# Two graph layers on one core: counts stored tile by tile, weights and count slabs on each other's queues, count ranges in pairs of chunks

## What is computed

```
edge_index = jnp.stack([src, dst])
x = _layernorm(x + graph_attention(x, W_fc, attn_l, attn_r, W_res, src, dst))
x = _layernorm(x + three_relational_layers(x, node_type, edge_index, edge_type, ...))

# attention, 12 heads of 64:   e = leaky_relu(a1[src] + a2[dst]); alpha = softmax of e over the edges of dst
#                              relu(x @ W_res + segment_sum(alpha * ft[src], dst))
# relational layer (3 times):  xw = h @ w_rel[r] for each relation r
#                              msg = xw[edge_type, src] / count[dst, edge_type]
#                              h = relu(segment_sum(msg, dst) + h @ w_root + bias)
```

## Time and profile before

| | |
|---|---|
| three runs | 2420.83, 2431.07, 2428.05 us; median 2428.05 |
| the profiled execution | 2421.66 us, span 2419.8 us |
| PE busy | 2181.1 us (90%) |
| DVE, ACT, POOL busy | 1225.3, 784.7, 461.4 us |
| moved by DMA | 215.26 MB in 138214 packets |
| mean granted TensorE clock | 0.959 |

### The profile page before, as it was taken

The page is one execution under the profiler, slowest core; times in us unless marked ns, Lnnn a source line. Parts: engine busy times, 40 slices in busy tenths (PEclk is TensorE's granted clock), DMA queues, the critical chain, the costliest instruction groups (busy, mean ns, idle before and its releaser), DMA issues.

```text
span 2419.8 us, 29974 instructions
## 1 busy us (share of the span) xinstructions
PE 2181.1 (90%) x10968; PEld 1835.2 (76%) x10969; DVE 1225.3 (51%) x1875; ACT 784.7 (32%) x1071; POOL 461.4 (19%) x389
## 2 busy tenths in 40 slices
PE   6999853888887599999999999999999899999997
PEld 2555531333333499999999899999999899999997
DVE  7888767999976633322322432322322342343335
ACT  1133334888885321211211421211211321212212
POOL 0000003999998000000000000000000000000000
PEclk8999975999998699999999999999999999999998
DMA  1134423211110433333432423333333423345332
GB/s 50 45 87 105 105 61 94 76 33 33 33 35 16 137 105 103 111 108 92 115 98 86 120 63 104 111 101 91 116 91 92 131 66 116 105 114 140 99 98 76
DMA packets 138214, 215.26 MB, mean 89 GB/s; under 512 B 87760, under 2 KB 87998, under 8 KB 138073
## 3 DMA queue, kind: packets, MB, share of 16 engines
q1 hardware_dynamic: 97187, 141.08, 20.7%
q0 software_dynamic: 40144, 70.00, 10.1%
q10 hardware_dynamic: 767, 2.57, 0.3%
HBM read 182.51 MB, written 30.70 MB: 88 GB/s over the span
## 4 chain that ended last, share of the span: by engine, by line
PE 59%; DMA 4%; DVE 3%; ACT 1%; issue 0%; ACTq 0%; DVEq 0%
PE banks L1193 30%; PE banks L1165 28%; DMA w_raw<-in_L_gnn_w_root_dram 4%; DVE w_lo L1413 1%; ACT w_hi L1295 1%; PE banks L1217 1%; PE banks L1204 0%; DVE norm_stats L1385 0%; DVE res L1381 0%; PE banks L1235 0%; DVE h_lo L1444 0%; ACT accT L1324 0%; DVE tail_stats L1464 0%; DVE back L1462 0%; ACT accT L1286 0%
## 5 line engine op out<-in xcount | busy, mean ns | idle before, releaser
L1165 PE MATMUL banks<-ct_in,h_hi 125*128 125x416 f32 (+1 forms) x1710 | 603.7, 353 | 0.6 <-ACT accT L1286 0.6
L1165 PE MATMUL banks<-ct_in,h_lo 125*128 125x416 f32 (+1 forms) x1710 | 602.5, 352 | 0.0
L1193 PE MATMUL banks<-g_hi,w_hi 128*128 128x416 f32 (+1 forms) x1440 | 516.5, 359 | 22.5 <-DVE g_lo L1435 22.5
L1193 PE MATMUL banks<-g_hi,w_lo 128*128 128x416 f32 (+1 forms) x1440 | 513.8, 357 | 0.0
L1193 PE MATMUL banks<-g_lo,w_hi 128*128 128x416 f32 (+1 forms) x1440 | 511.2, 355 | 0.0
L1413 DVE TENSOR_TENSOR w_lo<-w_raw,w_hi 128x768 fp32r<-128x768 f32 (+1 forms) x228 | 227.9, 1000 | 474.7 <-ACT w_hi L1295 474.7
L1295 ACT CAST w_hi<-w_raw 128x768 fp32r<-128x768 f32 (+1 forms) x228 | 198.0, 868 | 466.0 <-PE banks L1193 353.7
L939 PE MATMUL head_sums<-pw,x 125*65 125x512 f32 x720 | 274.2, 532 | 59.9 <-POOL pw L723 44.1
L1165 PEld LDWEIGHTS banks<-ct_in,h_lo 125*128 125x128 f32 x1710 | 323.1, 189 | 4.1
L1165 PEld LDWEIGHTS banks<-ct_in,h_hi 125*128 125x128 f32 x1710 | 321.7, 188 | 4.3 <-ACT accT L1286 0.8
L1311 ACT CAST g_hi<-gs 128x416 fp32r<-128x416 f32 (+3 forms) x180 | 97.4, 541 | 700.1 <-DVE gs L1423 700.1
(11 more groups left out here) (198 smaller groups left out, 1565.6 us busy)
## 6 DMA issues: line engine op xcount, KB each, us to landing
w_raw<-in_L_gnn_w_rel_dram SPq DMA_DIRECT2D x117, 384.0 KB, 3.1
ct_in<-s_ct POOLq DMA_DIRECT2D x18, 2031.2 KB, 28.2
w_raw<-in_L_gnn_w_rel_dram SPq DMA_DIRECT2D x54, 448.0 KB, 4.5
ct_in<-s_ct POOLq DMA_DIRECT2D x9, 2041.0 KB, 28.7
s_ct<-ct_stage SPq DMA_DIRECT2D x30, 610.4 KB
w_raw<-in_L_gnn_w_root_dram SPq DMA_DIRECT2D x39, 384.0 KB, 3.1
w_raw<-in_L_gnn_w_root_dram SPq DMA_DIRECT2D x18, 448.0 KB, 5.3
low_spread<-s_low SPq DMA_DIRECT2D x11, 610.4 KB
```

The lines of the kernel that those rows point to most:

```text
L1165: ins = nc.tensor.matmul(pb[0:rows, PA, 0:s.w], a, b, start=j == 0, stop=j == len(pairs) - 1)
L1193: ins = nc.tensor.matmul(pb[:, m, 0:s.w], a, b, start=s.first and j == 0, stop=s.last and j == len(parts) - 1)
```

## The change

It has three parts, in one diff.

1. Ranges begin at pairs of chunks. NPAIR = 160 pairs take the place of NRUN = 80 runs in the table. A pass of the loop still takes four chunks, now pairs q and q + 1, and the loop steps by 2; `ranges` rounds the number of pairs up to an even one, at least 2, with seven more small instructions. `oh_rem` is built in the same 20 instructions, with 2 in place of 4 as its innermost size. `hit` now lies in `csf`.
2. Counts are kept tile by tile: `dram["ct"]` is (R, NT, T, NT, T), relation, tile of destinations, partition, source tile, destination. A store writes 5000 contiguous bytes for each partition. A load of a slab is cut into PIECES = 4 transfers, one for each tile of destinations that the group touches; each still has 125 partitions by ten pieces of up to 125 numbers (500 bytes). All stores but those of the last tile are now issued in the count stage itself.
3. In the relational layers the queues are exchanged. POOL issues the weights, SP the slabs. SP stores four tiles of x1, then issues slab 0, stores four more, waits, issues slab 1, stores the last two; later each slab at the first step of the slab before it, in one order with the late loads and stores of x1.

```
@@ -27,9 +27,9 @@
...
-REM_R = 4
+REM_R = 8
...
-NRUN = NCH // CG
+NPAIR = NCH // 2
...
@@ -81,16 +81,16 @@
...
-        hit = sb("hits", [NW, 3, NRUN], F32)
-        rng = sb("ranges", [NW, 4], F32)
+        hit = csf[0:NW].rearrange("w s d -> w (s d)")[:, 0:3 * NPAIR].rearrange("w (m i) -> w m i", m=3)
+        rng = sb("ranges", [NW, 6], F32)
...
-        oh_rem = sb("oh_rem", [CH, NRUN, LANES, CG], BF16)
+        oh_rem = sb("oh_rem", [CH, NPAIR, LANES, 2], BF16)
...
@@ -134,10 +134,10 @@
...
-            return (nc.s_assert_within(eng.snap(both >> 7), 0, NRUN - 1, skip_runtime_bounds_check_because=WITHIN),
-                    nc.s_assert_within(eng.snap(both & 127), 1, NRUN, skip_runtime_bounds_check_because=WITHIN))
+            return (nc.s_assert_within(eng.snap(both >> 8), 0, NPAIR - 2, skip_runtime_bounds_check_because=WITHIN),
+                    nc.s_assert_within(eng.snap(both & 255), 1, NPAIR - 1, skip_runtime_bounds_check_because=WITHIN))
...
@@ -161,25 +161,24 @@
             with nc.allow_non_contiguous_dma(reason="100 numbers"):
                 sp.dma_start(tabf[:], rng[:, 2:3]).then_inc(tab_in, 16)
 
-            def tile(tt, b, kept=0):
+            def tile(tt, b, last=False):
                 g = tt * 2 + b
                 sp.wait_ge(rows_split, g * 2 + 2)
                 for m in range(2):
                     sp.dma_start(a_rows[m * H:(m + 1) * H, bass.ds(g * T, T)], splitrow[:, m]).then_inc(rows_out, 16)
-                if kept < R:
-                    tile_staged(sp, tt, b)
-                for r in range(R - kept):
-                    sp.dma_start(dram["ct"][r].rearrange("(s p) (u c d) -> p s u c d", p=T, c=2, d=T)[:, :, bass.ds(tt, 1), b].rearrange(
-                        "p s u d -> p s (u d)"), stage[0:T, b, r]).then_inc(stored[b], 16)
-                if not kept:
-                    sp.dma_start(dram["deg"][bass.ds(g, 1), :],
-                                 stage[T:T + 1, b].rearrange("a r s d -> a (r s d)")).then_inc(stored[b], 16)
+                if last:
+                    return
+                tile_staged(sp, tt, b)
+                for r in range(R):
+                    sp.dma_start(dram["ct"][r, bass.ds(g, 1)].rearrange("a p s d -> (a p) s d"), stage[0:T, b, r]).then_inc(stored[b], 16)
+                sp.dma_start(dram["deg"][bass.ds(g, 1), :],
+                             stage[T:T + 1, b].rearrange("a r s d -> a (r s d)")).then_inc(stored[b], 16)
 
             with sp.Fori(0, NT // 2 - 1) as tt:
                 tile(tt, 0)
                 tile(tt, 1)
-            tile(NT // 2 - 1, 0, kept=2)
-            tile(NT // 2 - 1, 1, kept=3)
+            tile(NT // 2 - 1, 0)
+            tile(NT // 2 - 1, 1, last=True)
             sp.wait_ge(rows_out, 32 * NT)
 
         @block.gpsimd
@@ -273,23 +272,35 @@
...
+                lo, hi, n = (rng[:, j:j + 1] for j in (0, 1, 4))
+                nc.vector.tensor_scalar(hi, rng[:, 2:3], 1.0, None, ALU.max).then_inc(dv, 1)
+                nc.vector.tensor_scalar(lo, rng[:, 3:4], -1.0, float(NPAIR), ALU.mult, ALU.add).then_inc(dv, 1)
...
+                nc.vector.scalar_tensor_tensor(out=lo, in0=hi, scalar=-1.0, in1=lo, op0=ALU.add, op1=ALU.min).then_inc(dv, 1)
...
+                nc.vector.tensor_tensor(n, hi, lo, ALU.subtract).then_inc(dv, 1)
...
+                nc.vector.tensor_scalar(n, n, 0.5, 0.25, ALU.mult, ALU.add).then_inc(dv, 1)
...
+                nc.vector.tensor_scalar(n, n, MAGIC, None, ALU.add).then_inc(dv, 1)
...
+                nc.vector.tensor_scalar(n, n, -MAGIC, 2.0, ALU.add, ALU.mult).then_inc(dv, 1)
...
+                nc.vector.tensor_tensor(hi, hi, n, ALU.max).then_inc(dv, 1)
...
+                nc.vector.tensor_tensor(lo, hi, n, ALU.subtract).then_inc(dv, 1)
...
+                nc.vector.scalar_tensor_tensor(out=rng[:, 2:3], in0=lo, scalar=256.0, in1=hi,
...
-                                        rem16[:, i * CG:(i + REM_R) * CG].rearrange("e (q c) -> e q c", c=CG)[:, :, None]
...
+            for i in range(0, NPAIR, REM_R):
+                nc.vector.tensor_tensor(oh_rem[:, i:i + REM_R, 0:T, :], iota_rem[:, None].to_broadcast([CH, REM_R, T, 2]),
+                                        rem16[:, i * 2:(i + REM_R) * 2].rearrange("e (q c) -> e q c", c=2)[:, :, None]
+                                        .to_broadcast([CH, REM_R, T, 2]), ALU.is_equal).then_inc(rem_ready, 1)
...
-            nc.vector.tensor_copy(tab[:], tabf[:]).then_inc(tab_ready, 1)
+            nc.vector.tensor_scalar(tab[:], tabf[:], -1.0, None, ALU.add).then_inc(tab_ready, 1)
...
@@ -299,11 +310,11 @@
...
-                with dve.Fori(*run_range(dve, w)) as q:
+                with dve.Fori(*run_range(dve, w), 2) as q:
...
-                        c = q * CG + b
+                        c = q * 2 + b
...
@@ -484,12 +495,12 @@
...
-                with pe.Fori(lo, hi) as q:
+                with pe.Fori(lo, hi, 2) as q:
...
-                            ins = nc.tensor.matmul(win[:, p, m, 0:BANK * KEY], oh_rem[:, bass.ds(q, 1), :, b].rearrange("e q s -> e (q s)"),
+                            ins = nc.tensor.matmul(win[:, p, m, 0:BANK * KEY], oh_rem[:, bass.ds(q + b // 2, 1), :, b % 2].rearrange("e q s -> e (q s)"),
...
@@ -650,12 +661,10 @@
...
-            for b, kept in ((0, 2), (1, 3)):
-                g = NT - 2 + b
-                for r in range(R - kept, R):
-                    sp.dma_start(dram["ct"][r].rearrange("(s p) d -> p s d", p=T)[:, :, g * T:(g + 1) * T],
-                                 stage[0:T, b, r]).then_inc(stored[b], 16)
-                sp.dma_start(dram["deg"][g:g + 1, :], stage[T:T + 1, b].rearrange("a r s d -> a (r s d)")).then_inc(stored[b], 16)
+            g = NT - 1
+            for r in range(R):
+                sp.dma_start(dram["ct"][r, g], stage[0:T, 1, r]).then_inc(stored[1], 16)
+            sp.dma_start(dram["deg"][g:g + 1, :], stage[T:T + 1, 1].rearrange("a r s d -> a (r s d)")).then_inc(stored[1], 16)
...
                 sp.dma_start(nt[:], io["node_type_3"].rearrange("(t p) -> p t", p=T)).then_inc(small_in, 16)
...
@@ -1014,8 +1023,9 @@
 OUT_ODD = [sum(m // 2 for m in MTS[:j]) for j in range(len(MTS) + 1)]
 LAST = STEPS[-1]
...
+TILES_OF = [range(o // T, (o + w - 1) // T + 1) for o, w in ROWS]
+PIECES = len(TILES_OF[0])
 X1_GROUP = [0] * 3 + [1] * (NT - 5) + [2] * 2
-X1_STORES = {1: (0, 1), 2: (2, 3), 4: (4, 5), 6: (6, 7), 8: (8, 9)}
...
@@ -1091,17 +1101,31 @@
...
-            for j, s in enumerate(W_STEPS):
+            def load(j):
+                s = SLABS[j][0]
...
-                    sp.wait_ge(w_lo_done, j - 1)
-                sp.dma_start(w_raw[:, j % 2, 0:s.mt * 128], weights_of(s)).then_inc(w_in[j % 2], 16)
-                if j == 2:
-                    sp.wait_ge(emb_zero, 1)
-                    for c in range(3):
-                        sp.dma_start(emb_w[c * 32:c * 32 + R].bitcast(F32), dram["emb"][c % 2]).then_inc(emb_in, 16)
-                if j in X1_STORES:
-                    for t in X1_STORES[j]:
-                        store_x1(t)
+                    sp.wait_ge(gs_done, SLABS[j - 2][-1].ai + 1)
+                sp.dma_start(inv[:, j % 2, 0:s.w], dram["inv"][s.r:s.r + 1, s.o:s.o + s.w].to_broadcast([128, s.w])
+                             ).then_inc(inv_in[j % 2], 16)
+                for t in TILES_OF[s.g]:
+                    lo, hi = max(s.o, t * T), min(s.o + s.w, (t + 1) * T)
+                    sp.dma_start(ct[j % 2][:, :, lo - s.o:hi - s.o].bitcast(F32),
+                                 dram["ct"][s.r, t, :, :, lo - t * T:hi - t * T]).then_inc(ct_in[j % 2], 16)
...
+            for t in range(4):
+                store_x1(t)
+            load(0)
+            for t in range(4, NT - 2):
+                store_x1(t)
+            sp.wait_ge(x1_out[1], 16 * X1_GROUP.count(1))
+            sp.wait_ge(xt_turned, 2 * (NT - 2))
+            sp.wait_ge(h_lo_done, NT - 2)
+            load(1)
+            for t in range(NT - 2, NT):
+                store_x1(t)
+            for s in STEPS:
+                if s.slab and s is SLABS[s.slab][0] and s.slab + 1 < len(SLABS):
+                    load(s.slab + 1)
...
@@ -1120,28 +1144,25 @@
...
+            def load_w(j):
+                s = W_STEPS[j]
+                if j >= 2:
+                    pool.wait_ge(w_lo_done, j - 1)
+                pool.dma_start(w_raw[:, j % 2, 0:s.mt * 128], weights_of(s)).then_inc(w_in[j % 2], 16)
...
+            load_w(0)
+            load_w(1)
...
-            def load(j):
-                s = SLABS[j][0]
-                if j >= 2:
-                    pool.wait_ge(gs_done, SLABS[j - 2][-1].ai + 1)
-                pool.dma_start(inv[:, j % 2, 0:s.w], dram["inv"][s.r:s.r + 1, s.o:s.o + s.w].to_broadcast([128, s.w])
-                               ).then_inc(inv_in[j % 2], 16)
-                pool.dma_start(ct[j % 2][:, :, 0:s.w].bitcast(F32),
```

(22 more changed lines are left out.)

30 lines of the change are left out of this document (14 added, 16 removed).

## The result

The changed kernel takes 2371.55 us (median of four runs, 2369.16 to 2373.51) beside 2429.34 for the kernel before on the same chip: a ratio of 0.9769, 95% interval 0.9743 to 0.9794. A later series on another occasion gave 0.9790 (0.9775 to 0.9805): 2373.25 beside 2423.97. The forecast was 2369, by a gain of 59 us; the two series show 57.8 and 50.7.

The account below looks back on a forecast made before the run. PE was taken to bound the relational stage, DVE's passes and SP's stores the count stage, POOL the attention heads. Gains of 24 + 16 + 6 + 13 = 59 us off a median of 2428 gave 2369, range 2347 to 2390.

Parts of the forecast that it names:

- Ranges: Count stage: nine passes fewer save 14.4 us at 1.6 us each, less 1.8 us for extra range instructions.
- that rival: Count stage: `oh_rem` halves its rate with the smaller inner size, + 21 us, time 2390; chance 0.06.
- Stores in the count stage: Count stage: long-row stores stop pacing the late tiles, 11.4 of the 24 us predicted for the stage.
- if the late tiles stay at 25 us: Count stage: stated sign that the prediction is wrong; it expected tiles 20 to 24 us apart from tile 3 on.
- 7.8 + 1.6 per pass: Count stage: formula for a tile's time in us; ten tiles with 120 passes give 270.0 us.
- The lower bound of 14: Count stage: smallest gain in us, if other limits hold late tiles at 22 to 23 us; 24 was forecast.
- Start of attention: Attention's beginning: the 21.01 us wait for last stores goes, POOL starts 18.7 us earlier; term 16, bounds 8 and 19.
- The 2.7 given back: Attention heads: 2.7 us of POOL's 18.7 us earlier start lost, as DVE has made fewer scores ahead.
- Relational beginning: Start of relational stage: weights 2 and 3 no longer queue behind x1 stores; 6 us, bounds 0 and 10.
- Root runs: Relational stage's short root steps: weights from POOL land earlier beside slabs, less PE idle; 13 us, bounds 0 and 27.
- The exchange gives nothing: Relational stage: rival that exchanging queues wins nothing, as all issuers share the same engines; time 2388, chance 0.19.
- Slabs: Relational stage: slabs in pieces land in 28 to 36 us, hidden, priced at 0; rival that they bound, chance 0.07.

Follow-up runs that it names:

- run 1: Only the ranges in pairs put into the kernel before; 0.9978 of that kernel's time, last eviction 12.1 us earlier.
- run 4: The changed kernel with ranges again in runs of four chunks (layout and exchange kept); 2382.81 us, 0.9834 of the kernel before.
- run 5: The changed kernel with the count stage's stores cut to a third; last eviction at 322.56 us, against 326.1 in the changed kernel's profile.
- run 6: The changed kernel with the count stage's attention scores made from one input block instead of six, less PE work; last eviction at 318.42 us.
- run 3: Only the queues exchanged in the kernel before: whole slabs from SP, weights from POOL; 2405.04 us, 0.9920 of the kernel before.
- run 7: The changed kernel with every slab loaded twice, the second time after the first has landed; 2562.68 us.
- run 9: The changed kernel with 418 one-hots: passes of four chunks, plus two behind a branch for an odd number of pairs; 0.9793 of the kernel before.
- run 8: The changed kernel with passes of two chunks instead of four, so two one-hot buffers in use; 1.0152 of the kernel before.

## Why the prediction was right, and which terms were not

The time and the sign were right, in part by errors of both signs and by some luck. The 59 us stand beside 57.8 in the first series, but the median of before there, 2429.34, is 3 to 5 us above that of four later and larger series (2423.97 to 2425.86); the later series gives 50.7. By stage, with the mean of all profiled executions that have the same code there, the count stage won 14.9 us for 24, attention 14 for 16, and the relational stage 25 for 19. The one pair of profiles below has 14.0, 10.0 and 24.4.

**Ranges: right.** 14.4 less 1.8 were predicted; 12.1 us (run 1) and 11.6 (run 4). One-hot group x480 with the same mean of 475 ns. `oh_rem` did not slow down, so that rival falls.

**Stores in the count stage: the mis-sized term.** 11.4 of the 24 us rested on "there SP is full" as the cause of late tiles 25 us apart. The stores did hold ACT (16.8 us before, nothing after), but taking that away brought 2.7 us in the mean, 1.5 to 4.5 by single executions: tiles 4 to 7 are still 24.4 to 27.0 us apart without long stores. That is the prediction's own sign of being wrong ("if the late tiles stay at 25 us"), and for this term it was. The price "7.8 + 1.6 per pass" was read from early tiles, where it fits; in a late one PE is busy 21.7 and DVE 19.0 of 24.6 us, and neither alone sets the pace (runs 5 and 6). The lower bound of 14 for the whole stage names such a case ("if other limits hold the late tiles at 22 to 23 us"), but the tiles came later than that, so that 14.0 was measured does not confirm it.

**Start of attention: right, giving back too small.** 18.7 us were predicted between the stage's end and POOL's first product, and 65.8 - 48.1 = 17.7 came. The sign given for it, a first product about 40 us earlier, had 24 of these from the count stage, so 31.7 came. The 2.7 given back were 4.4 in the first head (33.4 for 29.0 us). In this pair 3.3 more lie in heads that vary from run to run, so 16 was 10 here; over three executions with the old layout (mean 442.7 us from the last eviction to the end of attention) and eleven with the new one (428.7) it is 14.

**Relational beginning: too large.** 6 predicted, 2.5 measured. PE's waits on `x_tiles` and `x_more`, which are for DVE's norms, were 11.2 and 10.3 us and are 11.9 and 8.4: they stay.

**Root runs: too small, and the clock's sign was wrong.** The prediction had 57% of 23.9 us of idle time and let the clock take some back. Idle fell by 15.7, of which the wait for `g_lo`, the one the term is about, has 13.8, near the 13.6; and the clock added 6.3 where the prediction had it take back 0.6. Over the whole stage the old code has PE busy 1561.2 and 1567.0 us, the new one 1555.2 to 1557.8. In the stretch that answers to the earlier trace rows PE's clock is 0.98 for 0.93 and its idle time 5.3 for 9.7 us:

```profile
1832.00:1907.00 75.00, 69.72 (x374) 66.52 (x373) 33.46 (x52) 28.48 (x52) 7.52 (x14) 0.98 0.40 111
```

The weights' landing beside a slab was forecast below 7 us from one pair of rows. It is 6.0 at most in this stretch, where the same stretch before has 10.3, and 6.6 at most from 865 us on:

```profile
DMA to landing us min/median/max: 2.9/4.1/10.3
DMA to landing us min/median/max: 3.2/4.9/6.0
```

**The exchange gives nothing: refuted**, by run 3 (15 us for the exchange alone). The Trainium skill's "DMA: Bandwidth & Descriptors", section "Issuing engines are not separate DMA queues", has all issuers' transfers on the same 16 engines, and that part agrees with the rows: weights are late beside a slab from either side. That another issuer saves issue time alone does not agree with run 3; the measurement decides. The rows also show that the issuer matters for how much of the engines is taken at once: a share of 0.83 for 24 us from POOL and 0.48 for 30 us from SP, weights included, for the same four pieces. With the old queues the layout would have been a loss of 18 us in this stage, a risk that the prediction priced only as slabs landing late, not as weights landing late beside them.

**Slabs: right.** Landing about 30 us (30.2 in run 7, the 30 us of the stretch shown in the changed kernel), hidden; PE never waits for `ct_in` in the changed kernel, and run 7 shows what it costs past the cover. The stores' stretch was as forecast (share 0.32, 116 GB/s):

```profile
102.50:105.00 2.50, 2.29 (x14) 1.01 (x13) 2.04 (x6) 0.00 (x0) 0.00 (x0) 1.00 0.32 116
```

Left open: which part of a late tile's 3 us beyond PE's work is the hand-over of windows and which is PE's sequencer. Runs 5, 6 and 9 change the stores, PE's work and DVE's work, and none removes it. Left open too: what makes the tiles before the last longer with the new layout. Why the exchanged queues still beat pieces in turn on POOL by 14 us (1629.3 against 1615.1) was argued from the landings (9.6 against 6.0 us at most), not isolated.

## What to carry to other kernels

A queue that is full, even one that another engine waits for, is not yet the one that paces: ask what the next engine's busy time in that very stretch leaves. Here freeing SP won 3 us and not 11, with PE busy 21.7 and DVE 19.0 of 24.6 us in a late tile. Before a few microseconds are given to a cause, look at how far the same stage varies between executions of the same code: 3 us in the count stage here, more than what run 5 had to show. When a transfer is cut into pieces, look at how many are in flight at once and who shares the engines; a wait between pieces, on an engine with nothing else to do, was worth 28 us on POOL and nothing on SP. And count a stall with its clock: 15.7 us of idle time taken from PE came with 6.3 us less busy time, and the 160.5 us of waits in run 7 with 36 us more.

## What was not expected of the hardware

The same four pieces run side by side from POOL's queue (share 0.83, 24 us) and hardly so from SP's (0.48, 30 us, and 0.42 over 32 us with the waits between them), although the program has no wait between them.

PE's clock fell in two late tiles right after a gap, and those two tiles (27.0 and 25.4 us) are 3.2 us each above the formula, the three other late ones 0.6 to 1.1. In the first, PE is busy 0.90 of 2.5 us, and in the next 2.5 us the granted clock is 0.60:

```profile
187.50:190.00 2.50, 0.90 (x7) 0.57 (x8) 0.84 (x4) 0.41 (x1) 0.55 (x1) 1.00 0.60 171
190.00:192.50 2.50, 2.50 (x11) 1.22 (x10) 2.50 (x5) 0.00 (x0) 0.00 (x0) 0.60 0.44 149
```

With only two buffers between them DVE and PE each stand idle 0.4 us for every two one-hots (run 8), and with a branch in each window DVE was idle as much longer (23.1 us) as 62 one-hots fewer had made it busy shorter (22.4; run 9).
